# Second feed-forward of a two-layer kernel: first scales and down words loaded in attention's end, expansions of the first hidden tile moved ahead of its relu

## The reference

```python
w_up = ((w_up_q - 7.5) * repeat(w_up_scale, 64)).T            # 512 x 2048
y1 = x1 @ w_up + b_up + x1 @ w_up_lora_a @ w_up_lora_b        # rank 16
x2 = relu(y1)
w_down = ((w_down_q - 7.5) * repeat(w_down_scale, 64)).T      # 2048 x 512
y2 = x2 @ w_down + b_down + x2 @ w_down_lora_a @ w_down_lora_b
x = x + s * silu(y2)
```

## Time and profile before

| | us |
|---|---|
| median of three runs | 1745.63 |
| profiled execution | 1743.57 |
| its span, first to last instruction | 1741.8 |
| TensorE busy | 1637.5 (94%) |
| VectorE busy | 1179.6 (68%) |
| GpSimd busy | 620.0 (36%) |
| ScalarE busy | 393.8 (23%) |
| mean TensorE clock granted | 0.974 of full speed |

### The profile page before, as it was taken

How to read it: one execution, slowest core, us unless ns; L and a number is a source line. 1 busy time by engine, 2 the same in 40 slices (tenths; PEclk the granted TensorE clock), 3 DMA queues, 4 the chain that set the end, 5 groups by cost and what they waited for, 6 DMA issues and landing times. The chain is left out here.

```text
span 1741.8 us, 20345 instructions
## 1 busy us (share of the span) xinstructions
PE 1637.5 (94%) x6704; PEld 1133.8 (65%) x6704; DVE 1179.6 (68%) x1693; ACT 393.8 (23%) x670; POOL 620.0 (36%) x456
## 2 busy tenths in 40 slices
PE   6899868899999999989999999999998899999997
PEld 3444436547646656548877777777776567888886
DVE  6999867677878778746536877788776466242423
ACT  1222220011021110122223333333332222121211
POOL 3686543445554565450012222222322342010001
PEclk9999988999999999989999999999999899999999
DMA  5524658666676765513120000000003532202010
GB/s 200 193 108 167 246 174 236 214 210 207 214 218 206 225 208 190 194 55 103 47 75 25 19 24 14 25 19 19 19 1 111 162 109 98 79 19 78 12 61 24
DMA packets 85412, 200.49 MB, mean 115 GB/s; under 512 B 6864, under 2 KB 29136, under 8 KB 77008
## 3 DMA queue, kind: packets, MB, share of 16 engines
q1 hardware_dynamic: 85328, 199.42, 34.5%
HBM read 156.41 MB, written 42.99 MB: 114 GB/s over the span
## 5 line engine op out<-in xcount | busy, mean ns | idle before, releaser
L1029 POOL TENSOR_TENSOR r_rS<-r_S,r_rT 128x512 f32<-128x512 f32 x128 | 185.1, 1448 | 201.6 <-DVE r_S L1124 201.0
L1909 DVE SCALAR_TENSOR_TENSOR l_acc<-l_ps,l_inv,l_acc 128x512 f32<-128x512 f32 x240 | 167.3, 749 | 10.1 <-PE l_ps L725 10.1
L2435 DVE CAST g_x_part<-g_x 128x512 fp32r<-128x512 f32 x64 | 36.7, 573 | 195.2 <-ACT g_x L2486 195.2
L1124 DVE TENSOR_TENSOR_SCAN r_S<-r_dT,r_ps 128x512 f32<-128x512 f32 x128 | 156.4, 1222 | 17.3 <-POOL r_rS L1029 13.2
L1495 PE MATMUL r_ps<-Wdn,r_h 128*128 128x512 f32 x352 | 154.6, 595 | 0.0
L723 PE MATMUL r_ps<-relay_part,entry 128*128 128x512 f32 x256 | 108.0, 422 | 20.9 <-DVEq L1310 14.7
L1787 POOL TENSOR_TENSOR relay<-l_expq,l_reluq 128x512 f32<-128x512 f32 x42 | 54.3, 1294 | 192.4 <-ACT l_expq L2067 192.4
L1495 PEld LDWEIGHTS r_ps<-Wdn,r_h 128*128 128x128 f32 x352 | 65.7, 190 | 85.5 <-issue 85.4
L2363 POOL TENSOR_TENSOR relay<-relay 128x512 f32<-128x512 f32 x16 | 21.7, 1355 | 257.1 <-DVE relay L2413 257.1
L1885 DVE TENSOR_SCALAR l_expq<-l_ps,l_bq 128x512 f32<-128x512 f32 x64 | 48.0, 750 | 90.5 <-ACT l_reluq L2063 88.5
L723 PE MATMUL l_ps<-l_M_part,l_sq_part 128*128 128x512 f32 x256 | 101.6, 397 | 3.9 <-DVE l_acc L1909 3.1
(11 more groups left out here) (288 smaller groups left out, 3910.7 us busy)
## 6 DMA issues: line engine op xcount, KB each, us to landing
entry<-scratch_wgu SPq DMA_DIRECT2D x32, 1024.0 KB, 6.5
r_V<-scratch_v SPq DMA_DIRECT2D x96, 256.0 KB
relay<-scratch_x SPq DMA_DIRECT2D x15, 1024.0 KB, 7.4
r_w_part<-scratch_wgu SPq DMA_DIRECT2D x12, 1024.0 KB, 8.7
scratch_wgu<-f_halves SPq DMA_DIRECT2D x28, 384.0 KB, 4.3
relay<-scratch_v SPq DMA_DIRECT2D x32, 256.0 KB
relay<-in_x SPq DMA_DIRECT2D x4, 1024.0 KB, 8.4
scratch_x<-f_xT SPq DMA_DIRECT2D x4, 1024.0 KB, 6.8
```

Of the source, the lines that this page charges most:

```text
L1029: nc.gpsimd.tensor_tensor(rS[u % RS][:, :], S[u % 2][:, 0:T], rT[u // DK][:, :], ALU.mult).then_inc(rS_ready.sem, 1)
L1124: nc.vector.tensor_tensor_scan(S[u % 2][:, 1:T + 1], dT[hh][:, :], kv, 0.0, ALU.mult, ALU.add).then_inc(S_ready.sem, 1)
L1909: last = nc.vector.scalar_tensor_tensor(acc[b][:, t, :], ps, scale, acc[b][:, t, :], ALU.mult, ALU.add)
L2435: nc.vector.tensor_copy(hi[:, :], x2[j % 2][:, :]).then_inc(x2_hi_ready.sem, 1)
```

## The change

The edits in `linear_attention`: after the last q product, SP issues the two halves of up scale 1, down scales 0 and 1, and down words 0, and counts them in the same semaphore that hands over x and the up words (`hand`, which `relu_gate` receives as `handed`; nine transfers instead of two). To have room for them, their buffers share the places of `x_part[3][0]` and `Wq_part[0][0]`; some other allocations are made earlier, so that they lie elsewhere. In `relu_gate`: these loads go; `b_up` and `b_dn` stay; the expansions of j = 0 come ahead of its relu (ScalarE) and split (VectorE), and their low-rank products ahead of U(0); ScalarE waits for `b_up` behind its copies; VectorE counts `x_lo_ready` first; the two tensors `Wdn` become one with both parts side by side, and ScalarE waits for the stores of `s` before it writes down tile 6.

```diff
+        x_part = [kept["x_part"]] + [[sb(f"x_part{i}{b}", [P, KT, T], F32R) for i in range(2)] for b in range(1, B - 1)]
+        x_part += [[kept["x_last"], sb(f"x_part1{B - 1}", [P, KT, T], F32R)]]
+        Wq_part = [[kept["Wq_first"] if i == j == 0 else sb(f"Wq_part{i}{j}", [P, KT, D], F32R) for i in range(2)]
+                   for j in range(2)]
...
             sp.dma_start(flat(relay[2][:, :, :]), slab(spill["x2"], 1)).then_inc(hand, 16)
+            sp.wait_ge(*product("q", UNITS - 1))
+            for a in range(2):
+                rows_a = slice(64 * a, 64 * a + 64)
+                sp.dma_start(kept["next_scale"][rows_a, :],
+                             w["up_scale"][:, C:2 * C].unsqueeze(1).broadcast_to([8, 8, C])).then_inc(hand, 16)
+                for j in range(2):
+                    sp.dma_start(kept["dn_scale"][j][rows_a, :],
+                                 w["dn_scale1"][2 * j + a:2 * j + a + 1, :].broadcast_to([64, C])).then_inc(hand, 16)
+            sp.dma_start(flat(kept["dn_words"][:, :, :]), w["dn_q"][:, 0:2 * C]).then_inc(hand, 16)
...
+    S_UNDER = 6
...
-        Wdn = [sb(f"Wdn{i}", [P, UT, C], F32R) for i in range(2)]
+        Wdn = sb("Wdn", [P, UT, 2, C], F32R)
...
-        z = [kept["scale"], sb("z1", [P, C])]
-        tanh_z = [sb(f"tanh_z{i}", [P, C]) for i in range(2)]
+        z = [kept["scale"], kept["next_scale"]]
+        tanh_z = kept["dn_scale"]
...
             sp.dma_start(b_up[:, :], w["b_up"]).then_inc(b_up_loaded, 16)
-            load_up_scale(1)
-            load_down(0)
-            load_down_scale(0)
-            load_down_scale(1)
             sp.dma_start(b_dn[:, :], w["b_dn"]).then_inc(b_dn_loaded, 16)
 
-            sp.wait_ge(handed, 2 * 16)
+            sp.wait_ge(handed, 9 * 16)
             sp.sem_inc(up_loaded, 2 * 16)
-            sp.sem_inc(up_scale_loaded[0], 2 * 16)
+            sp.sem_inc(dn_loaded, 16)
+            for i in range(2):
+                sp.sem_inc(up_scale_loaded[i], 2 * 16)
+                sp.sem_inc(dn_scale_loaded[i], 2 * 16)
...
         def _(dve):
-            for q in (x_lo_ready, x2_hi_ready, x2_lo_ready, z_ready, u_ready, sg_ready):
+            x_lo_ready.ahead(dve)
+            dve.sem_inc(x_lo_ready.sem, KT)
+            for q in (x2_hi_ready, x2_lo_ready, z_ready, u_ready, sg_ready):
                 q.ahead(dve)
...
                 for j in range(UT):
-                    if first and j > 0:
+                    if first:
                         for x in tiles_at(j):
                             expand(x)
...
-                    if first and j == 0:
-                        for x in tiles_at(j):
-                            expand(x)
...
             def high(x):
...
+                if x == ("dn", S_UNDER):
+
+                    act.wait_ge(s_late, 16 * B)
...
                     act.sem_inc(x_hi_ready.sem, KT)
-                    act.wait_ge(b_up_loaded, 16)
...
-                    if first and j > 0:
+                    if first:
                         for x in tiles_at(j):
                             high(x)
+                        if j == 0:
+                            act.wait_ge(b_up_loaded, 16)
...
                     pre = tiles_at(n) if first and n < UT else []
+                    while pre and n == 0:
+                        make(pre.pop(0))
```

More of the change, by code:

```diff
@@ L1593, in linear_attention @@
         xT = kept["xT"]
-        x_part = [kept["x_part"]] + [[sb(f"x_part{i}{b}", [P, KT, T], F32R) for i in range(2)] for b in range(1, B)]
         wide, wide_hi, factors = relay[1], kept["up"][1], parts[1]
@@ L1600, in linear_attention @@
         whole = [bkv["k"], bkv["v"]]
-        kvT_part = [[sb(f"kvT_part{i}{b}", [P, KVH, D], F32R) for i in range(2)] for b in range(B)]
         ksum = [sb(f"ksum{b}", [P, KVH]) for b in range(B)]
[L1603 to L1606, removed]
         biased, expk = reluq, expq
@@ L2277, in load_down @@
             def load_down(c):
-                if c > 0:
-                    sp.wait_ge(expanded, 2 * number["dn", 2 * c - 1] + 1)
+                sp.wait_ge(expanded, 2 * number["dn", 2 * c - 1] + 1)
                 sp.dma_start(dn_q.rearrange("p a b -> p (a b)"), w["dn_q"][:, c * 2 * C:(c + 1) * 2 * C]).then_inc(
@@ L2283, in load_up_scale @@
             def load_up_scale(ob):
-                if ob >= 2:
-                    sp.wait_ge(expanded, 2 * number["up", ob - 2, KT - 1] + 1)
+                sp.wait_ge(expanded, 2 * number["up", ob - 2, KT - 1] + 1)
                 for a in range(2):
@@ L2291, in load_down_scale @@
             def load_down_scale(j):
-                if j >= 2:
-                    sp.wait_ge(expanded, 2 * number["dn", j - 2] + 1)
+                sp.wait_ge(expanded, 2 * number["dn", j - 2] + 1)
                 for a in range(2):
@@ L2351, in _ @@
                     continue
-                part = up_part(1, x[2], x[1] * C, C) if x[0] == "up" else Wdn[1][:, x[1], :]
-                high = up_part(0, x[2], x[1] * C, C) if x[0] == "up" else Wdn[0][:, x[1], :]
+                part = up_part(1, x[2], x[1] * C, C) if x[0] == "up" else Wdn[:, x[1], 1, :]
+                high = up_part(0, x[2], x[1] * C, C) if x[0] == "up" else Wdn[:, x[1], 0, :]
                 pool.wait_ge(w_hi_ready, i + 1)
@@ L2416, in sequence @@
             def sequence(b, first):
-                if first:
-                    dve.sem_inc(x_lo_ready.sem, KT)
-                else:
+                if not first:
                     dve.wait_ge(*U.product_before(("up", UT - 1), b))
@@ L2455, in high @@
             def high(x):
-                part = up_part(0, x[2], x[1] * C, C) if x[0] == "up" else Wdn[0][:, x[1], :]
+                part = up_part(0, x[2], x[1] * C, C) if x[0] == "up" else Wdn[:, x[1], 0, :]
+                if x == ("dn", S_UNDER):
+                    act.wait_ge(s_late, 16 * B)
                 act.wait_ge(expanded, 2 * number[x] + 2)
@@ L2487, in sequence @@
                                          bias=b_up[:, j:j + 1]).then_inc(x2_ready.sem, 1)
-                    if first and j == 0:
-                        for x in tiles_at(j):
-                            high(x)
             act.sem_inc(w_hi_ready, len(first_tiles))
@@ L2519, in down @@
                 return product3(nc, Y.place(("down", t))[:, :], [q[:, t * P:(t + 1) * P] for q in x2_part[i % 3]],
-                                [q[:, i, :] for q in Wdn], i == 0, i == UT - 1)
+                                [Wdn[:, i, part, :] for part in range(2)], i == 0, i == UT - 1)
             def sequence(b, first, last_batch=False):
@@ L2693, in stages @@
         kept["scale"] = sb("scale", [P, C])
+        with nc.sbuf_tensor("kept_x_last", [P, KT, T], F32R) as kept["x_last"]:
+            pass
+        kept["dn_words"] = sb("dn_words", [P, 2, C], I32)
+        kept["dn_scale"] = [sb(f"dn_scale{i}", [P, C]) for i in range(2)]
+        with nc.sbuf_tensor("kept_Wq_first", [P, KT, D], F32R) as kept["Wq_first"]:
+            pass
+        kept["next_scale"] = sb("next_scale", [P, C])
         with nc.sbuf_tensor("kept_narrow_part", [P, C], F32R) as kept["narrow_part"]:
```

6 lines of the change are left out of this document (5 added, 1 removed).

## The result

The changed kernel took 1727.84 us in the median of five runs (1725.26 to 1729.77), the kernel before 1744.08 beside it (1740.87 to 1749.09): a ratio of 0.9906, with a 95% interval of 0.9891 to 0.9920. The profiled execution took 1728.86, its span 1727.1 (before 1741.8).

The account below looks back on a forecast made before the run. TensorE was busy 94%, so time could be won only where it stands still, at the seam. 6.31 + 0.56 = 6.87 at VectorE, taken as 6.8: 1745.63 - 6.8 = 1738.8 us, range 1733 to 1744.

Parts of the forecast that it names:

- Addresses: New layouts: matmuls reading `g_Wup` and `g_Wdn` average 392 and 395 ns, so other places cost 0, bound 4 ns a matmul.
- Moved loads in attention, 0: Seven loads issued after the last q product cost attention 0, at most the 5.3 us of their issue.
- Expansions ahead of relu 0, cost 0: At the seam, the expansions of j = 0 start at about 1348 and finish before the relu at 1355.68: cost 0.
- Relu 0 where it was: The last stage's first relu stays at 1355.68, released by `b_up`; at most 2.4 us gained, 2 us late allowed.
- Rival A: The moved loads had held back `b_up` at the seam: up to 2.4 us more, gain 9.2, 1736.4 us; chance 0.17.
- 6.31 at the pair of j = 1: VectorE starts the expansions of j = 1 right after the split, at 1357.55 instead of 1363.86: 6.31 us earlier.
- A new wait at U4 of about 2.3: TensorE, early at the up product of hidden tile 4, waits some 2.3 us for GpSimd's fourth up tile.
- Rival B: The whole hole at the seam is won, tile four not holding U4: gain 10.8, 1734.8 us; chance 0.07.
- either way: Whether or not the wait at U4 drops the clock (1.7 us), U8 starts between 1401.7 and 1401.9.
- U8 6.7 to 6.9 earlier: The up product of hidden tile 8 starts at 1401.7 to 1401.9 instead of 1408.61, and the gain reaches the end.
- Rival C: Down matmuls reading the interleaved `Wdn` each take 25 ns more: 19.2 us lost, 1758.0 us; chance 0.05.
- D: The wait for `handed` ends later than 1355, a moved load landing behind the stores: no gain, 1745.6 us; chance 0.08.

Follow-up runs that it names:

- place_only: The kernel before with only attention's tensors allocated in the changed kernel's order, no load, wait or instruction moved: 1734.20 us, ratio 0.9952.
- x2_same_256: The changed kernel with 192 unused bytes behind `b_up` in the last stage, so `x2_part` starts at 128 modulo 256 like `Wdn`: 1721.41 us, ratio 0.9865.
- x_off64: The changed kernel with 64 unused bytes ahead of attention's x_part tensors and 64 behind: 1735.56 us, ratio 0.9961.
- x_misaligned: The changed kernel with 32 unused bytes ahead of attention's x_part tensors and 96 behind: 1735.11 us, ratio 0.9952.
- x_off128: The changed kernel with 128 unused bytes ahead of attention's x_part tensors and nothing behind: 1732.03 us, ratio 0.9924.
- b_up_first: The changed kernel with `b_up` loaded in attention's end and its 128 bytes allocated ahead of every tensor: 1726.11 us, ratio 0.9887.
- shift256: The changed kernel with 256 unused bytes ahead of attention's x_part tensors: 1726.94 us, ratio 0.9909.
- b_up_early: The changed kernel with `b_up` also loaded in attention's end, into 128 bytes behind the kept tensors: 1729.31 us, ratio 0.9911.

## Why the prediction was wrong, step by step

- **Addresses: wrong, and the step that failed.** The term was "0, with 4 ns a matmul as the bound either way". The places gave 9.3 us by place_only's time (1743.51 to 1734.20; its interval allows 4.7 to 12.2), and 9.5 from the first matmul of attention to its last in the two profiles (568.5 to 559.0 us). Of these 9.5, 2.8 stand ahead of the first relu of q and 6.7 behind it, in the heads. The size, 0.2333 to 0.2275 for q, is some 6 ns a matmul and above the bound of 4. But I multiplied the bound with nothing, because I looked for an effect only in matmuls that read `Wdn`, while the diff moved the tensors of attention, where TensorE has 2,599 matmuls from 776 to 1335: 4 ns on each would have been 10.4 us. And the 3 ns between `g_Wup` and `g_Wdn`, which I read as no effect of place, were this effect: the two tensors lie at one place, but `x2_part`, the other operand of the down ones, does not. From 1480 to 1590 down and up matmuls average 396 and 391 ns in the changed kernel and both 389 in x2_same_256.
- **The sum of the two.** 9.5 in attention and 6.6 at the seam are 16.1, beside 16.2 between the medians; that they agree so closely is in part luck, since single runs of one kernel spread over 4 to 8 us. The kernel before came out at 1744.08 in five runs instead of 1745.63 in three, which is another 1.6 of the 11.0 us between the forecast time and the measured one.
- **Moved loads in attention, 0: held.** Issued from 1309.73 to 1314.06 (7 in 4.3 us); from the relu of q of the 62nd unit to attention's last matmul, the stretch in which they run, it takes 39.66 us with them and 39.67 without (place_only).
- **Expansions ahead of relu 0, cost 0: held.** They began 3.5 us behind attention's last matmul (forecast 3.7), ended on VectorE at 1342.4, and it then idled 6.03 until relu 0.
- **Relu 0 where it was: held.** It stands 11.52 us behind attention's last matmul, 11.39 before; `b_up` took 9.3 from issue to landing, 9.2 before. Rival A fell.
- **6.31 at the pair of j = 1: 6.25.** It went from 1363.86 to 1349.53, 14.33, of which 8.08 are attention's.
- **A new wait at U4 of about 2.3: 2.17**, and no fall of the clock here. Rival B fell. In two runs with the same seam the clock did fall behind this wait: x_off64, after 2.16 us, has in the windows of the earlier trace rows

```profile
1364.69:1366.85 2.16, 0.01 (x1) 0.04 (x1) 1.28 (x2) 1.44 (x3) 1.38 (x2) 0.98 0.33 44
1366.90:1370.20 3.30, 3.30 (x8) 2.62 (x9) 1.74 (x2) 0.35 (x1) 1.14 (x1) 0.50 0.90 300
```

and x_misaligned, after 2.18, a clock of 0.50 from 1372.2 to 1375.6. U8 then waited 0.00 and 0.51 us instead of 1.12 and the end came as in the changed kernel (391.2 and 391.0 us behind attention's last matmul), so "either way" in the forecast was right.
- **U8 6.7 to 6.9 earlier: 7.44** against attention's last matmul (64.32 to 56.88). GpSimd's last up part came 7.46 earlier on that measure; up words 2 landed in 7.8 instead of 8.4, which is the 0.6. The wait at U8 was 1.12, not under 0.5, and U12 got one of 0.57, where the forecast had no more idle time behind U8, so the end kept 6.6. Place_only against the changed kernel gives 6.4 in time.
- **Rival C (longer down matmuls) and D (late hand-over) fell**: 395 ns as before; expansions at 1339.68.

So the mechanism at the seam was right, in place and in size, and a second effect of the same diff was priced at nothing.

## What to carry over

A diff that moves allocations changes the speed of code that it does not touch: list the first bytes of all tensors that TensorE reads, before and after, and price a difference between the two operands of a matmul over every matmul of the stage, by the mean distance between starts. Here a few dozen unused bytes that brought both operands to one place modulo 256 won 6.4 us in the last stage (x2_same_256), as much as the reworked seam. And in an experiment on layout, look at what lies behind a pad too: four runs agreed with a theory of 32 bytes that named the wrong quantity.

## What was not expected of the hardware

At a granted clock of 1.00, fp32r matmuls of 512 columns start 0.2267 to 0.2277 us apart in a layout where all operands share a place modulo 256, and up to 0.2304 where only their own two do; with operands whose places are 32, 64, 96 or 128 bytes apart it is 0.2313 to 0.2367. That each start is a multiple of 128 is not enough (x_off128), a common shift costs nothing (b_up_first), nor does a shift of some by 256 against others (shift256).

Single profiles of attention also differ by the clock at its opening. From 900 to 920 the granted clock was 0.91 in x_off128 and 1.00 in b_up_early, whose attention tensors lie at the same places, and from attention's first matmul to the 18th relu of q they took 226.6 and 223.3 us. The profiles of the kernel before and the changed one both had 0.91 there. The heads from the 18th unit on, at 1.00 in every profile, do not have this scatter.

The Trainium skill ("SBUF — State Buffer", Operand start alignment) asks of an operand's start only a multiple of its element size, and says that this is about legality, not speed, and that its runs timed nothing. All layouts here fulfil it, and their times differ all the same.

Open: the mechanism behind it, and why neighbours at one place lose 2 to 4 ns beside matmuls that are not (x2_same_256 also moved `whole` and `x2`, which VectorE and ScalarE write, so writes are not excluded there). Distances under 32 bytes, other data types and other column counts were not tried, nor whether the first layer's stages, whose tensors lie at many places, would gain.
